# Attention setup in a cross-attention and mixture-of-experts kernel: per-head matrices formed from 64-row operands instead of zero-padded 128-row blocks

## The chip, the cores and the metric

One core of one Trainium2 chip. The metric is the device time of one execution in microseconds. A core has TensorE (PE, matmuls), VectorE (DVE), ScalarE (ACT), GpSimd (POOL) and the DMA queues (SyncE issues most of them). TensorE writes its results to PSUM, eight banks of 128 partitions x 512 fp32; ScalarE and VectorE move them from there to SBUF.

## What is computed

```python
x = x + tanh(g_xattn[0]) * xattn(layernorm(x), ctx, Wq, Wk, Wv, Wo, bo)
x = x + tanh(g_ffn[0]) * ffn(layernorm(x), gate_w, w1, b1, w2, b2)
def xattn(x, context, Wq, Wk, Wv, Wo, bo):     # 16 heads of 64
    q = (x @ Wq); k = (context @ Wk * SCALE); v = (context @ Wv)
    attn = softmax(einsum('bihd,bjhd->bhij', q, k))
    return einsum('bhij,bjhd->bihd', attn, v).reshape(b, n, H * DH) @ Wo + bo
```

x is 2 x 1024 x 256, the context 2 x 64 x 256, everything fp32. The second part is a mixture of eight experts (256 to 1024 to 256, exact gelu), of which each batch element takes two, chosen from the mean of its rows.

## The kernel before

**Setup.** The kernel forms, once, two matrices that fold the projections into the context: A = Wq k^T, per head 256 x 64 for each batch element b, so that the scores are A^T xn; and VW = v Wo, per head 64 x 256 for each b, so that the output is the softmax times VW. The program calls these products *groups*, each of which fills one PSUM bank; `groups` gives their order: `ctxT` (the transposed context), `kT` 0 and 1, `wqT` 0 to 3 (transposes of Wq), `A` 0 to 7, `vT` 0 and 1, `VW` 0 to 7. Everything up to `A` 7 is called early. TensorE, ScalarE and VectorE each walk through this list in the same order (`group` in each engine's block). The early groups use the banks in turn, so that none of the A groups waits for a bank of another A group; the late ones (`vT`, `VW`) use banks 4, 5 and 6 in turn, and a group waits until the bank's previous group has been read (`GRP_BANK`, `GRP_BEFORE`, `wait_group_read`). For `VW` 0 to 7 the previous groups are `A` 7, `vT` 0, `vT` 1, `VW` 0, 1, 2, 3, 4.

**k and v.** A `kT` or `vT` group holds 128 rows (two heads of 64) x 4 head pairs x 2 batch elements x 64 positions. ScalarE evicts the even groups (L426), VectorE the odd ones (L621), each in two pieces of 64 partitions, into `kbd` and `vbd`: blocks of 128x128 of which one diagonal quarter holds head 0 of a pair and the other head 1. The rest is zero; GpSimd writes the zeros at the start (L350, L351), and the evictions wait for that (`zeros_ready`).

**A.** Group i covers half `ct = i // 4` of the 256 rows and two head pairs: two matmuls of a stationary 128x128 piece of `wqT` on a moving 128x256 piece of `kbd` (L936). ScalarE evicts a bank as `a_hi` (L439), rounded to fp32r; VectorE subtracts that from the bank and writes the rest as `a_lo` (L638). Ahead of the eviction of `A` 3 VectorE takes the statistics and the norm of the first half of x (L598 and L575 to L590).

**VW.** Group i covers batch element `b = i // 4` and two head pairs: two matmuls of a stationary 128x128 block of `vbd` on a moving 128x256 piece of `wo_sb` (L944). In the first group of each b a third matmul with one row adds the bias `bo` to head 0: `head0_row` (64 ones and 64 zeros) times `bo_row` (L949). ScalarE evicts the bank scaled by `tg` (L443), VectorE writes the rest (L644). VectorE takes the statistics of the second half of x ahead of `VW` 0.

**Steps.** After the early groups `run_steps` works on 16 tiles of 128 rows of x in a software pipeline: transposes of the normed tile (L1002), scores in three fp32r passes (L902 to L904), maximum (L693), exponentials (L488 and L471), sums (L680), reciprocal (L685), product on GpSimd (L366), transposes (L969), and the product with `vw`. The late groups stand between the steps for s = 0 and s = 1 (`value_groups`). On ScalarE the exponential of tile 0 (L471) comes behind the last `vw` eviction, and on VectorE the sum (L680) behind its own last one. The expert layers follow from 165 us on.

```python
if s == 1:
    value_groups()
...
dve.wait_ge(grp_hi, 8 + i + 1)
```

Of the kernel before, what the change touches and what calls it, by code (L numbers as in the profile page):

```python
# [5 lines left out]
def gated_cross_attention_moe_kernel(nc, x, ctx_tokens, g_xattn, g_ffn, Wq, Wk, Wv, Wo, bo,  # L6
# [5 lines left out]
    ALU = mybir.AluOpType  # L12
    ACT = mybir.ActivationFunctionType
# [3 lines left out]
    P = 128  # L17
    B, S, D = x.shape
    M = ctx_tokens.shape[1]
    HD = Wq.shape[1]  # L20
    DH = 64
# [6 lines left out]
    NP = HD // P  # L28
# [6 lines left out]
    SCALE = DH ** -0.5  # L35
# [46 lines left out]
    ones_row = place("ones_row", [1, P])  # L82
# [2 lines left out]
    b2sel = place("b2sel", [P, B, KD])  # L85
    swt = place("swt", [P, NQ])
    bo_row = place("bo_row", [1, D])
    head0_row = place("head0_row", [1, P])
    warm = place("warm", [1, 2])


# [3 lines left out]
    wv_sb = place("wv_sb", [P, KD, HD], at=first)  # L95
    wo_sb = place("wo_sb", [P, NP, D], at=first)
    wqT = place("wqT", [P, NP, D], at=first)
    kbd = place("kbd", [P, NP, B, P], at=first)
    vbd = place("vbd", [P, NP, B, P], at=first)
    ctx_sb = place("ctx_sb", [P, D], at=first)  # L100
    ctxT = place("ctxT", [P, KD, P], at=first)
    first2 = [cursor[0]]
# [39 lines left out]
    def as_f32(ap):  # L142
        return ap.bitcast(f32)

    stack = ExitStack()
    with stack:
# [99 lines left out]
        for kind, i in groups:  # L246
            who = "act" if kind in ("kT", "wqT", "vT") and i % 2 == 0 else "dve"
            counts[who] += 1
            reader[(kind, i)] = (who, counts[who])

        def wait_group_read(eng, kind, i):

            who, n = reader[(kind, i)]
            eng.wait_ge(grp_act if who == "act" else grp_dve, n)
# [89 lines left out]
        @block.gpsimd  # L344
        def _(pool):
            nc.gpsimd.memset(ident[:, :], 0.0).then_inc(zeros_ready, 1)
            pool.wait_ge(zeros_ready, 1)
            nc.gpsimd.affine_select(out=ident[:, :], in_=ident[:, :], compare_op=ALU.not_equal, fill=1.0,
                                    base=0, pattern=[[-1, P]], channel_multiplier=1).then_inc(ident_ready, 1)
            nc.gpsimd.memset(kbd[:, :, :, :], 0.0).then_inc(zeros_ready, 1)  # L350
            nc.gpsimd.memset(vbd[:, :, :, :], 0.0).then_inc(zeros_ready, 1)  # L351
            nc.gpsimd.memset(ones_row[:, :], 1.0)
            nc.gpsimd.memset(head0_row[:, 0:M], 1.0)
            nc.gpsimd.memset(head0_row[:, M:P], 0.0)
            for e in range(E):
                last = nc.gpsimd.memset(iota_row[:, e:e + 1], float(e))
            last.then_inc(rows_ready, 1)

            def step(s, par):
                t = s - 1  # L360
                if active(t):
                    q = (par - 1) % 2

                    pool.wait_ge(recip_done, t + 1)
                    pr = sx[:, q, :].rearrange("p (h m) -> p h m", m=M)
                    nc.gpsimd.tensor_tensor(pr, pr, rs[:, q, :].unsqueeze(2).broadcast_to([P, H, M]),  # L366
                                            ALU.mult).then_inc(mul_done, 1)
                t = s + LEAD
                if active(t):

                    wait_pos(pool, xT_done, t - 1)
                    tile = xt[:, ds(t, 1), :].rearrange("p o d -> p (o d)")
                    nc.gpsimd.tensor_tensor(xn[:, par, :], tile, mean1[:, ds(t, 1)].broadcast_to([P, D]),
                                            ALU.subtract).then_inc(xc_ready, 1)
                    pool.wait_ge(xc_ready, t + 1)
                    nc.gpsimd.tensor_tensor(xn[:, par, :], xn[:, par, :], rstd1[:, ds(t, 1)].broadcast_to([P, D]),
                                            ALU.mult).then_inc(xn_ready, 1)
            pool.wait_ge(ln_ready, 1)
            run_steps(pool, step)


            pool.wait_ge(ln_ready, 3)
            for t in range(TB, NT):
                pool.wait_ge(yT_done, t - 1)
                nc.gpsimd.tensor_tensor(yb[:, t % 2, :], xt[:, t, :], mean2[:, t:t + 1].broadcast_to([P, D]),
                                        ALU.subtract).then_inc(xc_ready, 1)
                pool.wait_ge(xc_ready, NT + t - TB + 1)
                nc.gpsimd.tensor_tensor(yb[:, t % 2, :], yb[:, t % 2, :], rstd2[:, t:t + 1].broadcast_to([P, D]),
                                        ALU.mult).then_inc(y_ready, 1)

        @block.scalar
        def _(act):
# [24 lines left out]
            def group(kind, i):  # L417
                n = number[(kind, i)]
                bank = ps[:, GRP_BANK[(kind, i)], :]
                if kind in ("kT", "vT") and i % 2 == 0:  # L420
                    act.wait_ge(grp_done, n + 1)
                    act.wait_ge(zeros_ready, 3)
                    dst = kbd if kind == "kT" else vbd
                    for h in range(2):
                        r = slice(h * DH, (h + 1) * DH)
                        last = nc.scalar.activation(  # L426
                            dst[r, 4 * i:4 * i + 4, :, h * M:(h + 1) * M],
                            bank[r, :].rearrange("p (m b j) -> p m b j", m=4, b=B), ACT.Copy,
                            scale=SCALE if kind == "kT" else 1.0)
                    last.then_inc(grp_act, 1)  # L430
                if kind == "wqT" and i % 2 == 0:
                    act.wait_ge(grp_done, n + 1)
                    nc.scalar.activation(wqT[:, 2 * i:2 * i + 2, :],
                                         bank.rearrange("p (m c) -> p m c", m=2), ACT.Copy).then_inc(grp_act, 1)
                if kind == "A":
                    act.wait_ge(grp_done, n + 1)
                    ct, mp = i // 4, i % 4
                    dst = a_hi[:, ct, :].rearrange("p (b m x) -> p m b x", b=B, x=P)[:, 2 * mp:2 * mp + 2, :, :]
                    nc.scalar.activation(dst, bank.rearrange("p (m b x) -> p m b x", m=2, b=B),  # L439
                                         ACT.Copy).then_inc(grp_hi, 1)  # L440
                if kind == "VW":
                    act.wait_ge(grp_done, n + 1)
# [115 lines left out]
        def _(dve):  # L558
# [50 lines left out]
            def group(kind, i):  # L609
# [4 lines left out]
                    nc.vector.tensor_copy(ctxT[:, :, :], bank[:, 0:D].rearrange("p (k i) -> p k i", k=KD)).then_inc(grp_dve, 1)  # L614
                if kind in ("kT", "vT") and i % 2 == 1:
                    dve.wait_ge(grp_done, n + 1)
                    dve.wait_ge(zeros_ready, 3)
                    dst = kbd if kind == "kT" else vbd
                    for h in range(2):
                        r = slice(h * DH, (h + 1) * DH)  # L620
                        last = nc.vector.tensor_scalar(  # L621
                            dst[r, 4 * i:4 * i + 4, :, h * M:(h + 1) * M],
                            bank[r, :].rearrange("p (m b j) -> p m b j", m=4, b=B),
                            SCALE if kind == "kT" else 1.0, None, ALU.mult)
                    last.then_inc(grp_dve, 1)
                if kind == "wqT" and i % 2 == 1:
                    dve.wait_ge(grp_done, n + 1)
                    nc.vector.tensor_copy(wqT[:, 2 * i:2 * i + 2, :],
# [2 lines left out]
                    x_stats(0)  # L631
                    x_norm(0)
                if kind == "A":
                    ct, mp = i // 4, i % 4
                    view = [w[:, ct, :].rearrange("p (b m x) -> p m b x", b=B, x=P)[:, 2 * mp:2 * mp + 2, :, :]
                            for w in (a_hi, a_lo)]
                    dve.wait_ge(grp_hi, i + 1)
                    nc.vector.tensor_tensor(view[1], bank.rearrange("p (m b x) -> p m b x", m=2, b=B),  # L638
                                            as_f32(view[0]), ALU.subtract).then_inc(grp_dve, 1)
                if kind == "VW" and i == 0:  # L640
                    x_stats(1)
                if kind == "VW":
# [253 lines left out]
        def _(pe):  # L896
# [9 lines left out]
            def group(kind, i):  # L906
# [17 lines left out]
                if kind == "wqT":  # L924
                    pe.wait_ge(ld_wq, 16)
                    for m in range(2):
                        for k in range(KD):
                            c0 = (2 * i + m) * P
                            last = nc.tensor.transpose(bank[:, (m * KD + k) * P:(m * KD + k + 1) * P],
                                                       wq_sb[:, k, c0:c0 + P], ident[:, :])  # L930
                if kind == "A":
                    ct, mp = i // 4, i % 4
                    wait_group_read(pe, "kT", mp // 2)
                    wait_group_read(pe, "wqT", mp)
                    for m in range(2):
                        last = mm(bank[:, m * B * P:(m + 1) * B * P], wqT[:, 2 * mp + m, ct * P:(ct + 1) * P],  # L936
                                  kbd[:, 2 * mp + m, :, :].rearrange("p b x -> p (b x)"), start=True, stop=True)
                if kind == "VW":
                    b, mp = i // 4, i % 4
                    pe.wait_ge(ld_wo, 16)  # L940
                    wait_group_read(pe, "vT", mp // 2)
                    for m in range(2):
                        biased = mp == 0 and m == 0
                        last = mm(bank[:, m * D:(m + 1) * D], vbd[:, 2 * mp + m, b, :], wo_sb[:, 2 * mp + m, :],  # L944
                                  start=True, stop=not biased)
                        if biased:
                            pe.wait_ge(rows_ready, 1)
                            pe.wait_ge(ld_small, 64)
                            last = mm(bank[:, 0:D], head0_row[:, :], bo_row[:, :], start=False, stop=True)  # L949
                last.then_inc(grp_done, 1)  # L950
            for g in groups[:EARLY]:
                group(*g)

            wait_group_read(pe, "A", 0)

            def value_groups():
                for g in groups[EARLY:]:
                    group(*g)

            def step(s, par):  # L960
                t = s - 2
# [215 lines left out]
```

## Time and profile before

| | us |
|---|---|
| three runs | 369.66, 371.54, 371.82 |
| median | 371.54 |
| the profiled execution | 371.07 |
| its span | 369.2 |
| setup up to TensorE's last A matmul | 22.5 |
| VW stage on TensorE | 38.4 to 47.4 |

The span runs from the first instruction to the last of the profiled execution. In the rows, `x16` is the count of merged instructions, the first number the start in us, the second the time they cover together. An fp32 matmul is two records. Names such as `a_hi` have their buffer number left out, and in `ps<-kbd,wqT 128*128 128x256` the first pair of numbers is the stationary operand, the second the moving one. The granted clock is a share of 2.4 GHz.

### The profile page before, as it was taken

Reading aid. Unit: us, or ns where it says so; the run is one execution under the profiler, and the core shown is the slowest. Engines: PE = TensorE matmul, PEld = TensorE weight load, DVE = VectorE, ACT = ScalarE, POOL = GpSimd, SP = SyncE. Lnnn points to the kernel's source line nnn. Section 1 sums busy time; section 2 is a strip of 40 time slices with the busy share of each in tenths; the row PEclk is TensorE's granted clock in tenths of the full one; section 3 lists DMA queues with packets and bytes.
Section 4 is the critical chain, followed back from the end, with each engine's and each line's share of the span. In section 5 each row is a group of like instructions: output and inputs, shape, how many; then the busy total and the mean of one; then the engine's idle time right before and its main releaser. Section 6 shows DMA issues by size and latency. Waiting matters only on the chain.

```text
span 369.2 us, 6051 instructions
## 1 busy us (share of the span) xinstructions
PE 339.2 (92%) x1782; PEld 285.5 (77%) x1782; DVE 240.6 (65%) x565; ACT 172.0 (47%) x583; POOL 65.5 (18%) x83
## 2 busy tenths in 40 slices
PE   1958889999999799879979999999999999999994
PEld 1937569989989599769858778888888888888883
DVE  0493789887688798865996882656566366552643
ACT  1433565766756477724355832435463264221420
POOL 5021034535445332210173000000000000000000
PEclk9987999999999899976999998999999999999998
DMA  6930000000000000052500076000000000020011
GB/s 209 369 119 2 1 7 0 2 0 0 0 0 0 1 3 0 2 176 73 210 0 0 2 235 221 2 0 0 0 0 2 1 0 0 17 99 0 1 58 57
DMA packets 12119, 17.22 MB, mean 47 GB/s; under 512 B 945, under 2 KB 10298, under 8 KB 12098
## 3 DMA queue, kind: packets, MB, share of 16 engines
q1 hardware_dynamic: 11536, 16.95, 13.8%
q8 instruction: 11, 0.18, 0.2%
q10 hardware_dynamic: 562, 0.01, 0.1%
q14 instruction: 10, 0.08, 0.1%
HBM read 14.86 MB, written 2.10 MB: 46 GB/s over the span
## 4 chain that ended last, share of the span: by engine, by line
PE 77%; DVE 13%; issue 3%; ACT 2%; DMA 2%; DVEq 1%; POOL 1%; SPq 0%
PE ps L902 22%; PE ps L904 21%; PE ps L903 21%; PE ps L969 4%; PE ps L922 2%; DMA wk_sb<-in_L_xattn_Wk_dram 2%; PE ps L1046 1%; DVE h_lo L866 1%; DVE h_hi L864 1%; PE ps L944 1%; DVE w_lo L877 1%; PE ps L1019 1%; PE ps L1106 1%; PE ps L1002 1%; DVE w_lo L872 1%
## 5 line engine op out<-in xcount | busy, mean ns | idle before, releaser
L532 ACT ACTIVATE gel<-ps,b1sel 128x512 f32<-128x512 f32 x64 | 44.0, 688 | 110.6 <-PE ps L904 110.5
L864 DVE CAST h_hi<-gel 128x512 fp32r<-128x512 f32 x64 | 28.0, 438 | 64.9 <-ACT gel L532 64.5
L902 PE MATMUL ps<-yT_hi,w_hi 128*128 128x512 f32 (+1 forms) x128 | 51.6, 403 | 0.0
L903 PE MATMUL ps<-yT_lo,w_hi 128*128 128x512 f32 (+1 forms) x128 | 51.3, 401 | 0.0
L904 PE MATMUL ps<-yT_hi,w_lo 128*128 128x512 f32 (+1 forms) x128 | 51.2, 400 | 0.0
L902 PE MATMUL ps<-h_hi,w_hi 128*128 128x512 f32 x128 | 50.9, 398 | 0.0
L904 PE MATMUL ps<-h_hi,w_lo 128*128 128x512 f32 x128 | 50.3, 393 | 0.0
L903 PE MATMUL ps<-h_lo,w_hi 128*128 128x512 f32 x128 | 50.3, 393 | 0.0
L866 DVE TENSOR_TENSOR h_lo<-gel,h_hi 128x512 fp32r<-128x512 f32 x64 | 45.5, 711 | 2.2
L366 POOL TENSOR_TENSOR sx<-sx,rs 128x1024 f32<-128x1024 f32 x16 | 30.5, 1904 | 81.7 <-DVE rs L685 81.7
L488 ACT ACTIVATE sx<-ps,mx 128x64 f32<-128x64 f32 x128 | 38.1, 323 | 13.9 <-DVE mx L693 13.9
L902 PE MATMUL ps<-vw,pT_hi 128*128 128x256 f32 (+1 forms) x128 | 38.5, 301 | 1.1 <-DVE pT_lo L671 1.1
L903 PE MATMUL ps<-vw,pT_hi 128*128 128x256 f32 (+1 forms) x128 | 37.1, 290 | 0.0
L904 PE MATMUL ps<-vw,pT_lo 128*128 128x256 f32 (+1 forms) x128 | 37.1, 290 | 0.0
L902 PE MATMUL ps<-a_hi,xT_hi 128*128 128x512 f32 (+1 forms) x64 | 28.0, 438 | 1.5 <-DVE xT_lo L699 1.5
L904 PEld LDWEIGHTS ps<-yT_hi,w_lo 128*128 128x128 f32 x128 | 24.5, 191 | 6.0
L903 PEld LDWEIGHTS ps<-yT_lo,w_hi 128*128 128x128 f32 x128 | 24.5, 191 | 5.5
L902 PEld LDWEIGHTS ps<-yT_hi,w_hi 128*128 128x128 f32 x128 | 24.3, 190 | 5.5
L903 PEld LDWEIGHTS ps<-h_lo,w_hi 128*128 128x128 f32 x128 | 24.1, 188 | 5.3
L902 PEld LDWEIGHTS ps<-h_hi,w_hi 128*128 128x128 f32 x128 | 24.1, 188 | 5.3
L904 PEld LDWEIGHTS ps<-h_hi,w_lo 128*128 128x128 f32 x128 | 24.0, 188 | 5.3
L488 ACT ACTIVATION_READ_ACCUMULATOR sx<-ps,mx 128x1 f32 x128 | 27.6, 215 | 0.0
(136 smaller groups left out, 627.6 us busy)
## 6 DMA issues: line engine op xcount, KB each, us to landing
stage_w<-in_L_ffn_w_dram SPq DMA_DIRECT2D x8, 1024.0 KB, 6.3
xt<-in_x_dram SPq DMA_DIRECT2D x2, 1024.0 KB, 13.0
out_dram<-xt SPq DMA_DIRECT2D x8, 256.0 KB, 2.1
wk_sb<-in_L_xattn_Wk_dram SPq DMA_DIRECT2D x1, 1024.0 KB, 7.2
wq_sb<-in_L_xattn_Wq_dram SPq DMA_DIRECT2D x1, 1024.0 KB, 9.5
wv_sb<-in_L_xattn_Wv_dram SPq DMA_DIRECT2D x1, 1024.0 KB, 14.0
wo_sb<-in_L_xattn_Wo_dram SPq DMA_DIRECT2D x1, 1024.0 KB, 12.1
ctx_sb<-in_ctx_dram SPq DMA_DIRECT2D x1, 128.0 KB, 3.2
```

What stands on the lines that cost most here:

```text
L366: nc.gpsimd.tensor_tensor(pr, pr, rs[:, q, :].unsqueeze(2).broadcast_to([P, H, M]), ALU.mult).then_inc(mul_done, 1)
L488: last = nc.scalar.activation(sx[:, par, c0:c0 + M], ps[:, 2 * par + 1, c0 - BANK:c0 - BANK + M], ACT.Exp, bias=mx[:, par, h:h + 1], accum ...
L532: nc.scalar.activation(gel[:, f % 2, :], ps[:, 4 + f % 2, :], ACT.Gelu, bias=b1sel[:, b, f, slot:slot + 1]).then_inc(gelu_done, 1)
L864: nc.vector.tensor_copy(h_hi[:, f % 4, :], gel[:, f % 2, :]).then_inc(hhi_ready, 1)
L866: nc.vector.tensor_tensor(h_lo[:, f % 4, :], gel[:, f % 2, :], as_f32(h_hi[:, f % 4, :]), ALU.subtract).then_inc(hlo_ready, 1)
L872: nc.vector.tensor_tensor(w1_lo[nxt][:, ds(pc, 1), pf * P:(pf + 1) * P], stage_w1[nxt][:, ds(pc, 1), pf * P:(pf + 1) * P], as_f32(w1_hi[nx ...
L877: nc.vector.scalar_tensor_tensor(w2_lo[nxt][:, pf, ds(pc * P, P)], stage_w2[nxt][:, pf, ds(pc * P, P)], swt[:, q + 1:q + 2], as_f32(w2_hi[ ...
L902: mm(acc, hi_w, hi_x, start=start, stop=False)
L903: mm(acc, hi_w, lo_x, start=False, stop=False)
L904: return mm(acc, lo_w, hi_x, start=False, stop=stop)
L922: last = mm(bank[:, m * P:(m + 1) * P], w_sb[:, k, c0:c0 + P], ctxT[:, k, :], start=(k == 0), stop=(k == KD - 1))
L969: last = nc.tensor.transpose(ps[:, 4 + half, m * P:(m + 1) * P], sx[:, par, c0:c0 + P], ident[:, :])
```

## The change

`kbd` and `vbd`, their zeros, the wait for these and `head0_row` are gone. k and v are evicted in one piece per bank into `kT_sb` and `vT_sb` (partitions 0 to 63 head 0 of each pair, 64 to 127 head 1). A and VW are formed per head: each matmul takes 64 rows, either 0 to 63 or 64 to 127. TensorE works on two groups at a time (`score_pair`, `value_pair`), of which the even one collects heads 0 of the pairs and the odd one heads 1, each in a bank of its own; in VW the two positions within a bank go to output partitions 0 to 63 and 64 to 127. A pair of groups waits for both of its banks first, and signals at its last matmul into either. The order of the heads within a batch element changes with it (`a_part`), the same way in A and VW. The groups, their banks and what each waits for are as before.

```diff
-    kbd = place("kbd", [P, NP, B, P], at=first)
-    vbd = place("vbd", [P, NP, B, P], at=first)
+    kT_sb = place("kT_sb", [P, NP, B, M], at=first)
+    vT_sb = place("vT_sb", [P, NP, B, M], at=first)
...
+        def a_part(w, i):
+
+            ct, half, odd = i // 4, i // 2 % 2, i % 2
+            return w[:, ct, :].rearrange("p (b u m x) -> p u m b x", b=B, u=4, x=M)[:, 2 * half + odd, :, :, :]
...
-            nc.gpsimd.memset(kbd[:, :, :, :], 0.0).then_inc(zeros_ready, 1)
-            nc.gpsimd.memset(vbd[:, :, :, :], 0.0).then_inc(zeros_ready, 1)
             nc.gpsimd.memset(ones_row[:, :], 1.0)
-            nc.gpsimd.memset(head0_row[:, 0:M], 1.0)
-            nc.gpsimd.memset(head0_row[:, M:P], 0.0)
...
                     act.wait_ge(grp_done, n + 1)
-                    act.wait_ge(zeros_ready, 3)
-                    dst = kbd if kind == "kT" else vbd
-                    for h in range(2):
-                        r = slice(h * DH, (h + 1) * DH)
-                        last = nc.scalar.activation(
-                            dst[r, 4 * i:4 * i + 4, :, h * M:(h + 1) * M],
-                            bank[r, :].rearrange("p (m b j) -> p m b j", m=4, b=B), ACT.Copy,
-                            scale=SCALE if kind == "kT" else 1.0)
-                    last.then_inc(grp_act, 1)
+                    dst = kT_sb if kind == "kT" else vT_sb
+                    nc.scalar.activation(dst[:, 4 * i:4 * i + 4, :, :].rearrange("p m b j -> p (m b j)"), bank, ACT.Copy,
+                                         scale=SCALE if kind == "kT" else 1.0).then_inc(grp_act, 1)
...
-                                            as_f32(view[0]), ALU.subtract).then_inc(grp_dve, 1)
+                    nc.vector.tensor_tensor(a_part(a_lo, i), bank.rearrange("p (m b x) -> p m b x", m=4, b=B),
+                                            as_f32(a_part(a_hi, i)), ALU.subtract).then_inc(grp_dve, 1)
...
-                if kind == "A":
-                    ct, mp = i // 4, i % 4
-                    wait_group_read(pe, "kT", mp // 2)
-                    wait_group_read(pe, "wqT", mp)
-                    for m in range(2):
-                        last = mm(bank[:, m * B * P:(m + 1) * B * P], wqT[:, 2 * mp + m, ct * P:(ct + 1) * P],
-                                  kbd[:, 2 * mp + m, :, :].rearrange("p b x -> p (b x)"), start=True, stop=True)
...
+            def two_banks(kind, i):
+
+                banks = []
+                for odd in range(2):
+                    banks.append(ps[:, GRP_BANK[(kind, i + odd)], :])
+                    if GRP_BEFORE[(kind, i + odd)]:
+                        wait_group_read(pe, *GRP_BEFORE[(kind, i + odd)])
+                return banks
+
+            def score_pair(i):
+
+                ct, half = i // 4, i // 2 % 2
+                banks = two_banks("A", i)
+                wait_group_read(pe, "kT", half)
+                wait_group_read(pe, "wqT", 2 * half)
+                wait_group_read(pe, "wqT", 2 * half + 1)
+                for m in range(4):
+                    for odd in range(2):
+                        r = slice(odd * DH, (odd + 1) * DH)
+                        last = mm(banks[odd][:, m * P:(m + 1) * P], wqT[r, 4 * half + m, ct * P:(ct + 1) * P],
+                                  kT_sb[r, 4 * half + m, :, :].rearrange("p b j -> p (b j)"), start=True, stop=True)
+                        if m == 3:
+                            last.then_inc(grp_done, 1)
+
+            def value_pair(i):
+
+                b, half = i // 4, i // 2 % 2
+                banks = two_banks("VW", i)
+                pe.wait_ge(ld_wo, 16)
+                wait_group_read(pe, "vT", half)
+                for c in range(2):
+                    for pos in range(2):
+                        m = 4 * half + 2 * c + pos
+                        for odd in range(2):
+                            r = slice(odd * DH, (odd + 1) * DH)
+                            biased = m == 0 and odd == 0
+                            last = mm(banks[odd][pos * M:(pos + 1) * M, c * D:(c + 1) * D], vT_sb[r, m, b, :],
+                                      wo_sb[r, m, :], start=True, stop=not biased)
+                            if c == 1 and pos == 1:
+                                last.then_inc(grp_done, 1)
+                    if half == 0 and c == 0:
+
+                        pe.wait_ge(rows_ready, 1)
+                        pe.wait_ge(ld_small, 64)
+                        mm(banks[0][0:M, 0:D], ones_row[:, 0:M], bo_row[:, :], start=False, stop=True)
```

VectorE's evictions of the odd `kT` and `vT` groups and ScalarE's of `a_hi` change in the same way.

## Rows read from the trace of the kernel before

**Rows 1.** The page, busy time by engine: us, share of the span, instructions.
```profile
PE 339.2 (92%) x1782; PEld 285.5 (77%) x1782; DVE 240.6 (65%) x565; ACT 172.0 (47%) x583; POOL 65.5 (18%) x83
```

**Rows 2.** Table by stretch: us, busy us (instructions) by engine, granted clock, DMA share, GB/s.
```profile
15.50:22.50 7.00, 6.99 (x33) 5.80 (x31) 6.09 (x16) 4.45 (x8) 0.00 (x0) 1.00 0.95 305
22.50:26.80 4.30, 0.00 (x0) 0.00 (x0) 3.71 (x19) 0.69 (x2) 1.29 (x3) 0.83 0.00 0
...
29.00:31.70 2.70, 2.70 (x7) 2.13 (x8) 0.00 (x0) 0.00 (x0) 0.26 (x1) 0.50 0.02 6
38.40:47.40 9.00, 8.73 (x35) 6.22 (x36) 7.27 (x15) 4.63 (x7) 0.00 (x0) 1.00 0.00 1
52.20:59.10 6.90, 6.85 (x46) 6.19 (x46) 6.08 (x18) 4.90 (x26) 3.13 (x4) 1.00 0.01 2
```

**Rows 3.** Chain that ended last, 8 to 53 us: start, us, what.
```profile
15.58 2.60 PE ps L936 x12
...
25.43 3.08 DVE a_lo L638 x5
...
44.50 3.34 PE ps L944 x14
...
49.25 0.69 DVE sm L680
...
50.29 1.91 POOL sx L366
52.25 0.76 PE ps L969 x5
```

**Rows 4.** Timeline, 0 to 20 us: start, us, engine, line, operation, count, [idle before].
```profile
1.43 1.80 POOL L350 MEMSET kbd<- 128x2048 f32 x1
...
12.08 1.19 ACT L426 ACTIVATE kbd<-ps 64x512 f32<-64x512 f32 x2 [6.28 <-PE ps L922]
...
13.67 1.91 PE L929 MATMUL ps<-ident,wq_sb 128*128 128x128 f32 x16
13.87 1.39 DVE L621 TENSOR_SCALAR kbd<-ps 64x512 f32<-64x512 f32 x2 [8.63 <-PE ps L922]
...
15.29 1.29 DVE L628 COPY wqT<-ps 128x512 f32<-128x512 f32 x2
...
15.41 7.07 PE L936 MATMUL ps<-kbd,wqT 128*128 128x256 f32 x32
...
18.20 0.60 ACT L439 ACTIVATE a_hi<-ps 128x512 fp32r<-128x512 f32 x1 [0.27 <-PE ps L936]
18.83 0.69 DVE L638 TENSOR_TENSOR a_lo<-ps,a_hi 128x512 fp32r<-128x512 f32 x1 [0.17 <-ACT a_hi L439]
...
19.44 2.70 DVE L598 BATCH_NORM_STATS2 stats<-xt  x8
```

**Rows 5.** Timeline, 37 to 49 us.
```profile
37.07 1.21 ACT L426 ACTIVATE vbd<-ps 64x512 f32<-64x512 f32 x2
...
38.42 0.67 PE L944 MATMUL ps<-wo_sb,vbd 128*128 128x256 f32 x2 [1.18 <-ACT vbd L426]
38.77 2.71 DVE L598 BATCH_NORM_STATS2 stats<-xt  x8
...
39.02 0.69 PE L949 MATMUL ps<-bo_row,head_row 1*128 1x256 f32 x2
...
39.65 2.43 PE L944 MATMUL ps<-wo_sb,vbd 128*128 128x256 f32 x10
...
42.32 1.56 PE L944 MATMUL ps<-wo_sb,vbd 128*128 128x256 f32 x6 [0.24 <-DVE vw L644]
43.48 0.69 ACT L443 ACTIVATE vw<-ps,tg 128x512 fp32r<-128x512 f32 x1 [0.69 <-PE ps L944]
...
48.58 0.75 DVE L644 SCALAR_TENSOR_TENSOR vw<-ps,tg,vw 128x512 fp32r<-128x512 f32 x1 [0.22 <-ACT vw L443]
```

**Rows 6.** Timeline of TensorE, 222 to 225 us: narrow moving operands.
```profile
222.69 1.94 PE L1046 MATMUL ps<-hotT,b_sb 8*128 8x2 f32 x16
```

More of the change, by code:

```diff
@@ L87, in gated_cross_attention_moe_kernel @@
     bo_row = place("bo_row", [1, D])
-    head0_row = place("head0_row", [1, P])
     warm = place("warm", [1, 2])
@@ L436, in group @@
                     act.wait_ge(grp_done, n + 1)
-                    ct, mp = i // 4, i % 4
-                    dst = a_hi[:, ct, :].rearrange("p (b m x) -> p m b x", b=B, x=P)[:, 2 * mp:2 * mp + 2, :, :]
-                    nc.scalar.activation(dst, bank.rearrange("p (m b x) -> p m b x", m=2, b=B),
+                    nc.scalar.activation(a_part(a_hi, i), bank.rearrange("p (m b x) -> p m b x", m=4, b=B),
                                          ACT.Copy).then_inc(grp_hi, 1)
@@ L616, in group @@
                     dve.wait_ge(grp_done, n + 1)
[L617 to L625, printed above, removed]
+                    dst = kT_sb if kind == "kT" else vT_sb
+                    nc.vector.tensor_scalar(dst[:, 4 * i:4 * i + 4, :, :].rearrange("p m b j -> p (m b j)"), bank,
+                                            SCALE if kind == "kT" else 1.0, None, ALU.mult).then_inc(grp_dve, 1)
                 if kind == "wqT" and i % 2 == 1:
@@ L633, in group @@
                 if kind == "A":
-                    ct, mp = i // 4, i % 4
-                    view = [w[:, ct, :].rearrange("p (b m x) -> p m b x", b=B, x=P)[:, 2 * mp:2 * mp + 2, :, :]
-                            for w in (a_hi, a_lo)]
                     dve.wait_ge(grp_hi, i + 1)
-                    nc.vector.tensor_tensor(view[1], bank.rearrange("p (m b x) -> p m b x", m=2, b=B),
-                                            as_f32(view[0]), ALU.subtract).then_inc(grp_dve, 1)
+                    nc.vector.tensor_tensor(a_part(a_lo, i), bank.rearrange("p (m b x) -> p m b x", m=4, b=B),
+                                            as_f32(a_part(a_hi, i)), ALU.subtract).then_inc(grp_dve, 1)
                 if kind == "VW" and i == 0:
@@ L930, in group @@
                                                        wq_sb[:, k, c0:c0 + P], ident[:, :])
-                if kind == "A":
-                    ct, mp = i // 4, i % 4
-                    wait_group_read(pe, "kT", mp // 2)
-                    wait_group_read(pe, "wqT", mp)
-                    for m in range(2):
-                        last = mm(bank[:, m * B * P:(m + 1) * B * P], wqT[:, 2 * mp + m, ct * P:(ct + 1) * P],
-                                  kbd[:, 2 * mp + m, :, :].rearrange("p b x -> p (b x)"), start=True, stop=True)
@@ L938, in group @@
[L938 to L949, printed above, removed]
@@ L951, in _ @@
             for g in groups[:EARLY]:
-                group(*g)
+                if g[0] != "A":
+                    group(*g)
+                elif g[1] % 2 == 0:
+                    score_pair(g[1])
             wait_group_read(pe, "A", 0)
@@ L957, in value_groups @@
                 for g in groups[EARLY:]:
-                    group(*g)
+                    if g[0] != "VW":
+                        group(*g)
+                    elif g[1] % 2 == 0:
+                        value_pair(g[1])
             def step(s, par):
```

## The prediction

> **What bounds the kernel now.** I read the page's engine shares first: TensorE is busy for 92% of the span [rows 1]. That is an average, and the change touches only the first 50 us, so the second view was the table by stage [rows 2]. There TensorE is full while A is formed (7.0 us of 7.0, 15.5 to 22.5 us), has no work at all for 4.3 us behind it, and is nearly full in the VW stage (8.7 of 9.0 us) and in the steady steps (6.85 of 6.9). Only the chain of waits says which of these stretches set the end [rows 3]. In the A stage the chain follows TensorE only through the first twelve records (each fp32 matmul is two records), then passes to VectorE: its third `a_lo`, the statistics and norm of the first half of x, and its five remaining `a_lo`, ending at 28.5 us. So the second half of the A matmuls lies beside VectorE's statistics and is on no path. In the VW stage the chain is TensorE's, and it leaves by the last `vw` eviction, VectorE's sum `sm`, GpSimd's product `sx`, and the transposes at 52.25 us. From there TensorE is full [rows 2], and a delay at that point is carried to the end one for one: TensorE, ScalarE and VectorE all take their work in order and have nothing else that they could draw forward.
>
> **Memsets.** Two of 1.80 us on GpSimd, over by 5 us, go [rows 4]. The first eviction that needed the zeros starts at 12.08 us [rows 4]. Worth 0.
>
> **k and v evictions.** Two pieces of 64x512 per bank become one of 128x512. A 64-partition piece takes ScalarE 1.19 / 2 = 0.60 us and VectorE 1.39 / 2 = 0.69 us; the 128-partition evictions of `a_hi` and `wqT` take the same 0.60 and 1.29 / 2 = 0.65 us [rows 4]. So partitions cost nothing, and a bank's eviction halves. For k this is off the path: the chain there is TensorE, from the k matmuls through the transposes [rows 4]. It lets VectorE take its `wqT` at 14.75 instead of 15.29 us, which the change needs, since the first pair of A groups waits for `wqT` 0 and 1. For v it is on the path: TensorE's first VW matmul waits for ScalarE's eviction, 37.07 to 38.28 us, and starts at 38.42 [rows 5]. After: 37.67, and 37.81 us. Gain 0.6 us there, and VectorE's statistics of the second half of x (2.71 us) move from 38.77 to 38.07 and end at 40.8. The long strides of the new `a_hi`/`a_lo` views cost nothing: the k eviction already writes runs of 64 elements at the full rate.
>
> **A.** Sixteen fp32 matmuls of 256 columns become 32 of 64 rows and 128 columns. Now: 7.07 / 32 = 0.22 us a record [rows 4]; a record of 128 columns costs half, 0.11. Two records of one matmul use the same rows of the array and must follow each other; but the second of one can run beside the first of the next, which uses the other rows. Then a matmul costs one record time, a pair of groups 8 x 0.11 = 0.9 us. What matters is when VectorE can begin its third `a_lo` (18.83 us now [rows 4]), since from there to its fourth at 25.43 it works without a gap. TensorE starts at 15.6 (15.41 and one change of the array's shape, 0.19, worked out below); the first pair's first bank is ready at 15.6 + 7 x 0.11 + 0.39 = 16.8 (0.39 from the start of its last record to ScalarE, which is the 0.49 found below for a record of 256 columns, less 0.1 for the shorter one); ScalarE then evicts three banks, 16.8, 17.4, 18.0, ending at 18.6. The second pair, held for `wqT` 3 until 16.3, is done by 17.7, in time. Third `a_lo` at 18.6: 0.2 us earlier. Below it is bounded by ScalarE, so no more than 0.2 can be won however fast TensorE is. Above: the trace has sixteen records that move only two columns and so show the pace of weight loads of 128 columns, 1.94 / 16 = 0.12 us [rows 6]. If two loads can't go at once, 64 loads are 7.7 us, the second pair starts at 17.5, its first bank is ready at 17.5 + 13 x 0.12 + 0.39 = 19.5, and the third `a_lo` starts at 20.1: 1.3 us later. I take -0.2, because the loads go into separate rows as the matmuls do, and keep +1.3 for the range.
> The Trainium skill, page "TensorEngine Tiling (Array Packing)", section "Key Properties", says that different tiles can load weights and multiply in parallel; by it the A term is the -0.2. No row here shows two tiles at work.
>
> **VW.** Sixteen matmuls of 256 columns (and two of the bias) become 32, on 64 rows and 64 columns each, in four quadrants. One record of 256 columns is 0.222 us, as in A. The four of group 3 start from 42.32, and ScalarE's eviction follows at 43.48 [rows 5]: 3 x 0.222, and 0.49 from the last record's start. Alone, one after another, the new 64 records are 14.2 us; all four quadrants at once 3.6 us. I take 7.1: quadrants are issued in program order, two records each, so that one matmul's second record overlaps the next one's first and no more. TensorE's sum is thus unchanged, and what decides is the order. The bias keeps its price, 2 x 0.213 and a pause on either side: from the first matmul's two records at 38.42 to the bias at 39.02 are 0.60 us, to the next at 39.65 another 0.63; two records fill 0.43 of each, and some 0.19 are left over each time [rows 5]. In all 0.81 us, at the first and third pair.
> A pair now fills two banks and both are finished only at its end, out of three banks. The pair (2,3) needs the bank of group 0, so it waits for VectorE's read of it; (4,5) for the read of 2; (6,7) for the read of 4. Before, group 3 waited for 0, 4 for 1 and so on, with the group between at work: TensorE waited 0.2 us there. Now nothing runs beside an eviction. From a pair's start: first bank ready for ScalarE after 7 x 0.222 + 0.49 = 2.05 (2.86 with bias); ScalarE 0.69 us, VectorE starts 0.03 behind it, 0.75 us, TensorE 0.06 later [rows 5].
> Pair 0: TensorE 37.81, ScalarE 40.7 and 41.4, VectorE 41.4 to 42.2. Pair 1: TensorE 42.2, ScalarE 44.3, VectorE 45.0 to 45.8. Pair 2: TensorE 45.8, ScalarE 48.7, VectorE 49.4 to 50.2. Pair 3: TensorE 50.2, ScalarE 52.3 and 53.0, the last `vw` on VectorE 53.7. It is at 48.58 now [rows 5]: +5.1 us. Pauses of TensorE of about 1.7 us stand between pairs.
> The Trainium skill, page "TensorE: Matmul & The Clock Gate", section "The mechanism" of Part 3, says that matmuls start and end in program order, without reordering; by it the VW sum stays 7.1, not 3.6. The page "TensorEngine Tiling (Array Packing)", "Key Properties", says that a change of tiling mode drains the engine; the trace agrees at the bias, 0.19 us each way.
>
> **Sum.** The profiled execution: 371.07 us, span 369.2. 371.07 - 0.2 + 5.1 = 376.0 us. The median of the runs, 371.54, lies 0.47 above it; on that scale 376.4. What measurement can tell from no change is about 1%, 3.7 us.
>
> **Rivals.**
> (a) Weight loads of two row groups don't overlap: A +1.3 instead of -0.2, 371.5 + 5.1 + 1.3 = 377.9 us. For it: the load pace of 0.12, the same for 8 rows as it would be for 64. Against: that pace is of loads into the same rows, where the second has to wait anyway.
> (b) Not slower: all four quadrants of VW work together. A pair's first bank is then ready after 0.67 + 0.49 = 1.16 us (1.97 with bias). VectorE reads group 0 at 40.8 (its statistics), the pairs start at 37.8, 41.6, 44.3 and 47.8, the last `vw` at 50.4, +1.8; with A -0.2, 373.1 us, inside 1%. It decides from the point where a pair takes TensorE under 1.2 us instead of 1.8. For it: each quadrant has cells and an output range of its own. Against: two records per matmul on the same quadrant, in order. To be level, a pair would have to cost almost nothing.
> (c) The change doesn't do what it says: narrow matmuls run one by one. VW 14.2 us: a pair's first bank after 13 x 0.222 + 0.49 = 3.4 us; the last `vw` at 59.0, +10.4; A +1.3: 383.2 us. For it: the trace shows no two matmuls at once.
> (d) The granted clock falls in the pauses of VW. It was 1.00 until TensorE had been idle for some 2.8 us, then 0.50 (a mean of 0.83 over 22.5 to 26.8 [rows 2]). The new pauses are 1.7 us. If it falls, three pairs take 7 x 0.21 = 1.5 us more each: 381 us.
> The first scores ran at 0.50 [rows 2] behind the idle time of the A stage; TensorE is idle there after the change as well, for longer, so I count 0, give or take 1 us for when the clock comes back.
>
> **How the numbers follow.** Forecast 42%, (a) 18%, (b) 20%, (c) 9%, (d) 4%, and 7% for a gain from something not seen here. The range 372.6 to 380.0 holds the forecast, (a) and (b). (c), (d) and the gain, 20%, are outside. The forecast's own range is 375.2 to 377.6. Slower by over 1% (above 375.3): the forecast less a small part, (a), (c), (d), 69%. Within 1%: (b) and that part, 24%. Faster: 7%.
>
> **What the profile would show.** Right: A's 64 records in about 4 us, with VectorE's third `a_lo` near 18.6; v evicted in 0.60 us; VW's first record near 37.8, TensorE waiting for VectorE's `vw` three times, 1.7 us each, and the last `vw` near 53.7; the steps behind it as long as now. Wrong: A over 7 us (a); 16 records of a VW pair within 1 us (b) or 3.5 us (c); a granted clock under 1.00 in VW (d). If TensorE doesn't wait for `vw` between the pairs, or the step behind VW absorbs the delay, the main term is wrong.

## The result and the profile after

376.72 us in the median of four runs, beside 371.3 for the kernel before on the same chip: ratio 1.0143, 95% interval 1.0098 to 1.0189. A second measurement, told below, gave 1.0126. The profiled execution took 377.56 us, the slowest of the four (the fastest took 376.0), its span 375.4. The forecast was 376.4, slower. The ratios leave out runs more than 1.5% above the fastest of the same kernel: that takes out five of the twelve runs of the group-by-group kernel below, which lie at 374.3 to 375.2 us, but not the similar ones of the kernel before, at about 374 (four of the 35 beside the first experiments, eight of the 23 beside the later ones), and no trace of such a run was kept.

The table by stretch of the kernel after (us, busy us and instructions of TensorE, its weight loads, VectorE, ScalarE, GpSimd, then granted clock, DMA share, GB/s):

```profile
44.00:46.00 2.00, 0.39 (x8) 0.22 (x8) 1.04 (x2) 1.26 (x2) 0.00 (x0) 0.65 0.00 0
46.00:50.00 4.00, 3.04 (x18) 0.69 (x15) 0.56 (x2) 0.91 (x2) 0.00 (x0) 0.50 0.01 4
50.00:54.00 4.00, 3.34 (x19) 2.04 (x20) 1.81 (x3) 1.67 (x4) 0.00 (x0) 0.50 0.02 8
```

Beside [rows 2]: TensorE is busy for 0.4 of 2 us and then for some 3 of 4 where it was nearly full, and the granted clock falls within the VW stage, from 1.00 to 0.50 (0.65 is the mean of the stretch in which it fell). It was 1.00 throughout that stage before.

The timeline of the kernel after, 12 to 56 us, all engines:

```profile
12.30 0.60 ACT L423 ACTIVATE kT_sb<-ps 128x512 f32<-128x512 f32 x1 [8.06 <-PE ps L905]
...
14.92 0.69 DVE L610 TENSOR_SCALAR kT_sb<-ps 128x512 f32<-128x512 f32 x1 [9.66 <-PE ps L905]
...
16.60 3.68 PEld L935 LDWEIGHTS ps<-kT_sb,wqT 64*128 64x128 f32 x64 [0.21 <-DVE wqT L614]
16.63 3.84 PE L935 MATMUL ps<-kT_sb,wqT 64*128 64x128 f32 x64
...
18.42 1.89 DVE L621 TENSOR_TENSOR a_lo<-ps,a_hi 128x512 fp32r<-128x512 f32 x3 [1.06 <-ACT a_hi L431]
20.23 2.70 DVE L590 BATCH_NORM_STATS2 stats<-xt  x8
...
38.53 0.64 ACT L423 ACTIVATE vT_sb<-ps 128x512 f32<-128x512 f32 x1
...
39.30 0.66 PE L952 MATMUL ps<-wo_sb,vT_sb 64*64 64x256 f32 x8 [0.62 <-ACT vT_sb L423]
...
39.90 0.64 PE L960 MATMUL ps<-bo_row,ones_row 1*64 1x256 f32 x2
...
41.18 1.27 ACT L435 ACTIVATE vw<-ps,tg 128x512 fp32r<-128x512 f32 x2 [2.02 <-PE ps L952]
...
43.10 1.09 PE L952 MATMUL ps<-wo_sb,vT_sb 64*64 64x256 f32 x16 [1.97 <-DVE vw L627]
44.24 1.26 ACT L435 ACTIVATE vw<-ps,tg 128x512 fp32r<-128x512 f32 x2 [1.79 <-PE ps L952]
44.96 1.41 DVE L627 SCALAR_TENSOR_TENSOR vw<-ps,tg,vw 128x512 fp32r<-128x512 f32 x2 [1.30 <-ACT vw L435]
...
45.81 1.13 PE L952 MATMUL ps<-wo_sb,vT_sb 64*64 64x256 f32 x8 [1.61 <-DVE vw L627]
...
49.09 1.27 ACT L435 ACTIVATE vw<-ps,tg 128x512 fp32r<-128x512 f32 x2 [3.59 <-PE ps L952]
...
50.66 1.98 PE L952 MATMUL ps<-wo_sb,vT_sb 64*64 64x256 f32 x16 [1.62 <-DVE vw L627]
...
53.41 1.41 DVE L627 SCALAR_TENSOR_TENSOR vw<-ps,tg,vw 128x512 fp32r<-128x512 f32 x2 [2.19 <-ACT vw L435]
```

k is evicted in 0.60 and 0.69 us instead of 1.19 and 1.39 [rows 4], v by ScalarE in 0.64 instead of 1.21 [rows 5]. A's 64 records take 3.84 us; its 32 of twice the columns took 7.07. The VW stage reads as a ladder: a pair on TensorE (43.10), two evictions by ScalarE (44.24), VectorE's two behind them (44.96), and, once the first of VectorE's two has read its bank, the next pair (45.81). From the first VW record to the last `vw` eviction it was 10.2 us (38.42 to 48.58 [rows 5]); now it is 14.8 (39.30 to 54.1, the second of the two that begin at 53.41).

The chain that ended last, of the kernel after, 8 to 60 us:

```profile
8.48 6.40 PE ps L905 x32
...
43.10 1.15 PE ps L952 x16
44.26 0.68 ACT vw L435
44.96 0.76 DVE vw L627
45.81 1.13 PE ps L952 x8
46.94 1.04 PE ps L960 x2
```

Between pairs it runs over ScalarE and VectorE, as forecast. Its first line is the k matmuls, 6.40 us. In the chain of the kernel before they took 5.33:

```profile
8.50 5.33 PE ps L922 x32
```

In both kernels TensorE's first records take twice the time of the later ones. Before, 14 of them stand in the 3.10 us from 8.50 on and 21 in the 2.10 us from 11.70 on; in this execution the slow ones reach to 13.80 (25 records in 5.30 us), and the k matmuls end 1.05 us later. That is no effect of the change (the second measurement's profiled execution has VectorE's k eviction at 14.05, 0.87 us earlier than this one), but it has to be taken off every time read here against before. A further 0.65 us stands in the first scores, which run at a granted clock of 0.50 at first in both kernels: from the first of them to the v matmuls it was 4.52 us (28.99 to 33.51), now it is 5.17 (29.78 to 34.95), and 4.73 in the second measurement's execution. The forecast counted 0 for it, give or take 1 us; whether the change has a part in it isn't shown.

Behind the last pair the chain doesn't leave as forecast, by the last `vw`. The second tile's scores stand behind that pair on TensorE, and the chain goes through them (at half clock at first) to VectorE's maximum of that tile. Its line in the chain of the kernel after, and the same maximum in the timeline of the kernel before:

```profile
56.67 1.24 DVE mx L676
```

```profile
50.63 1.23 DVE L693 TENSOR_REDUCE mx<-ps 128x16 f32<-128x1024 f32 x1 [0.42 <-PE ps L904]
```

This maximum is 6.04 us later than before. GpSimd's product of the first tile, which hangs on the last `vw`, is 5.48 later (55.77 against 50.29 [rows 3]). The maxima of the later tiles are 6.0 to 6.1 us late (the twelfth at 122.97 against 116.92), so what is carried to the end is the delay of the scores.

### The profile page after: what moved, and what is told of

It reads as the page before. It is cut to its first block, busy times and chain, and to the rows that moved or that the text cites. A ratio compares the mean times of both kernels' runs of the same rounds, so it can differ in the third digit from the quotient of the medians.

```text
span 375.4 us, 6169 instructions
## 1 busy us (share of the span) xinstructions
PE 338.4 (90%) x1846; PEld 282.4 (75%) x1846; DVE 238.7 (64%) x563; ACT 169.8 (45%) x581; POOL 61.8 (16%) x79
## 4 chain that ended last, share of the span: by engine, by line
PE 76%; DVE 14%; ACT 3%; issue 3%; DMA 2%; DVEq 1%; POOL 1%; SPq 0%
PE ps L885 21%; PE ps L886 21%; PE ps L887 21%; PE ps L985 3%; PE ps L905 3%; DMA wk_sb<-in_L_xattn_Wk_dram 2%; PE ps L952 1%; PE ps L1062 1%; DVE h_lo L849 1%; DVE h_hi L847 1%; ACT sx L480 1%; DVE a_lo L621 1%; DVE w_lo L860 1%; PE ps L1035 1%; DVE stats L590 1%
```

## The experiments

**A alone.** VW, v and its zeros stay as before; A is written in the old order of heads.

```diff
-            for g in groups[:EARLY]:
-                group(*g)
+            for g in groups[:EARLY]:
+                if g[0] != "A":
+                    group(*g)
+                elif g[1] % 2 == 0:
+                    score_pair(g[1])
```

> A formed as in the change (k evicted whole, no zero blocks for k, 64-row pairs), VW and v as before. Theory P (the whole loss is in the VW stage: pairs held back by three banks, and the clock that falls in their pauses): the third a_lo comes 0.2 to 0.3 us earlier relative to the k eviction, VW stage as before, so about 371.1 us, ratio 0.999. Rival R (the A part costs as well, because TensorE is idle for longer behind it and its clock comes back later in the first scores, 4.6 us instead of 2.9): 0.5 to 1.5 us slower than before, about 372.3 us, ratio 1.003.

Measured: 369.93 us beside 370.54, ratio 0.9991 (0.9954 to 1.0028). The timeline of this kernel, first VW matmul and last `vw`:

```profile
38.31 0.67 PE L944 MATMUL ps<-wo_sb,vbd 128*128 128x256 f32 x2 [1.19 <-ACT vbd L434]
...
48.47 0.75 DVE L651 SCALAR_TENSOR_TENSOR vw<-ps,tg,vw 128x512 fp32r<-128x512 f32 x1 [0.22 <-ACT vw L449]
```

Both 0.11 us earlier than in [rows 5]. The A part costs nothing in the trace and gives about what was forecast there; the interval doesn't exclude a gain or a loss of 1 us, but the loss of 5 us is elsewhere.

**VW group by group.** Everything of the change is kept, but the pair is split into its two groups, on the same three banks.

```diff
+            def value_one(i):
+                b, half, odd = i // 4, i // 2 % 2, i % 2
+                bank = ps[:, GRP_BANK[("VW", i)], :]
+                wait_group_read(pe, *GRP_BEFORE[("VW", i)])
...
-                    elif g[1] % 2 == 0:
-                        value_pair(g[1])
+                    else:
+                        value_one(g[1])
```

> The changed kernel, but VW formed group by group as before: the four matmuls of the even group, then those of the odd one, each signalled and waited for alone, on the same three banks and quadrants. Theory P: TensorE and the evictions overlap again; a group's four matmuls use two column halves of the same rows and take 0.9 us or less, so the stage is at least as fast as before, the v eviction saves 0.6 us: 370.3 us, ratio 0.998; granted clock 1.00 in the stage. Rival Q (64-row, 64-column fp32 matmuls and their changes of the array's shape are what costs): stays near 376 us.

Measured: 369.84 us beside 370.54, ratio 0.9956 (0.9929 to 0.9983), so the loss is gone. The profiled execution took 369.73 us, against 371.07 before. Its timeline:

```profile
38.32 0.65 PE L951 MATMUL ps<-wo_sb,vT_sb 64*64 64x256 f32 x4 [0.62 <-ACT vT_sb L423]
...
39.47 1.51 PE L951 MATMUL ps<-wo_sb,vT_sb 64*64 64x256 f32 x20
...
42.07 1.31 PE L951 MATMUL ps<-wo_sb,vT_sb 64*64 64x256 f32 x12 [1.09 <-DVE vw L627]
...
47.96 0.75 DVE L627 SCALAR_TENSOR_TENSOR vw<-ps,tg,vw 128x512 fp32r<-128x512 f32 x1 [0.59 <-ACT vw L435]
```

Twenty records follow each other from 39.47, through three groups, while ScalarE evicts; the stage is 9.6 us long (38.32 to 47.96) instead of 14.8, its granted clock 1.00. The 64-row matmuls and the quadrants are the same as in the changed kernel. So neither is what cost the time. It was the unit in which they were waited for, together with the clock that fell in the waits (Filler, below).

**Five banks.** The changed kernel, pairs and all, with two more banks for VW.

```diff
-        GRP_BANK = {g: n % 8 if n < EARLY else 4 + (n - EARLY) % 3 for n, g in enumerate(groups)}
+        LATE_BANKS = [4, 5] + [2, 3, 6, 4, 5, 2, 6, 4]
+        GRP_BANK = {g: n % 8 if n < EARLY else LATE_BANKS[n - EARLY] for n, g in enumerate(groups)}
...
+                if isinstance(s, int) and s == 1:
+                    wait_group_read(pe, "VW", 5)
```

> The changed kernel with VW's groups in five banks instead of three (2 to 6; the second tile's scores then wait for the read of group 5). Theory P: TensorE no longer waits for a pair's evictions, ScalarE's eight evictions of 0.64 to 0.69 us follow each other without a gap from 1.9 us after the stage's start and the last vw comes some 3 us earlier than in the kernel before: 368 us, ratio 0.991. Rival Q: 374 to 376 us.

Measured: 370.19 us beside 370.54, ratio 0.9982 (0.9957 to 1.0008). The loss is gone here too, by the other way of taking the wait out; a gain isn't shown. Its timeline:

```profile
37.69 0.66 PE L953 MATMUL ps<-wo_sb,vT_sb 64*64 64x256 f32 x8 [0.62 <-ACT vT_sb L424]
...
41.49 0.66 PE L953 MATMUL ps<-wo_sb,vT_sb 64*64 64x256 f32 x8 [1.11 <-DVE vw L628]
...
44.09 2.73 DVE L628 SCALAR_TENSOR_TENSOR vw<-ps,tg,vw 128x512 fp32r<-128x512 f32 x4 [0.72 <-ACT vw L436]
```

The last `vw` begins at 46.1 (the fourth of those from 44.09), 2.5 us earlier than before; I had expected some 3. The third pair still waits for the read of group 0, which comes behind VectorE's statistics. The profiled execution is faster by 2.1 us (368.99 beside 371.07), and the second tile's maximum is 2.0 earlier (48.61), but the median of twelve runs, from 368.13 to 371.58, is lower by only 0.35. What the other runs lost is open: only one of them has a trace.

**Filler.** The changed kernel with matmuls in the pauses, whose results nobody reads.

```diff
                         value_pair(g[1])
+                        if g[1] < 6:
+                            for _ in range(FILL):
+                                mm(ps[:, 3, :], xT_hi[:, 0, 0, :], a_hi[:, 0, 0:BANK], start=True, stop=True)
```

> The changed kernel with six more matmuls of 128x512 behind each of the first three VW pairs, into a bank that the next scores overwrite; they lie in TensorE's pauses of 2 us. Theory P with the clock: the granted clock stays 1.00 through the stage, pairs 2 and 3 and the second tile's scores run at full rate, 2 to 3 us less than the changed kernel: 374.2 us. Rival (the clock is beside the chain): no less than the changed kernel, 376.7 us, or more by the changes of shape.

Measured: 373.54 us beside 370.54, ratio 1.0065 (1.0034 to 1.0095). More work made the kernel faster, by about 2.5 us against the changed one (1.0143 and 1.0126 against 1.0065). Its timeline, and its table by stretch:

```profile
41.38 1.09 PE L953 MATMUL ps<-wo_sb,vT_sb 64*64 64x256 f32 x16 [0.39 <-DVE vw L628]
...
42.40 1.66 PE L978 MATMUL ps<-a_hi,xT_hi 128*128 128x512 f32 x6
...
47.54 1.09 PE L953 MATMUL ps<-wo_sb,vT_sb 64*64 64x256 f32 x16
...
49.40 1.41 DVE L628 SCALAR_TENSOR_TENSOR vw<-ps,tg,vw 128x512 fp32r<-128x512 f32 x2 [1.30 <-ACT vw L436]
```

```profile
38.00:46.00 8.00, 7.58 (x64) 3.88 (x58) 5.21 (x12) 2.56 (x5) 0.00 (x0) 1.00 0.00 1
46.00:52.00 6.00, 5.76 (x36) 3.94 (x36) 3.98 (x7) 3.18 (x6) 0.23 (x1) 1.00 0.04 11
```

The filler (1.66 us) ends before the next pair may start, so it changes no wait; pairs take 1.09 us, the last one too (1.98 in the changed kernel), and the clock is granted at 1.00 throughout. What is left, 2.4 us over the kernel before (1.3 to 3.5 by the interval), is the ladder at full clock. The profiled execution, the fastest of the twelve, has less of it: the last `vw` is at 50.1 us, 1.5 behind [rows 5], and the second tile's maximum at 51.63, 1.0 behind.

**Quadrant by quadrant.** The changed kernel with the loops inside a pair turned; the bias stands directly behind the matmul that it is added to.

```diff
-                for m in range(4):
-                    for odd in range(2):
+                for odd in range(2):
+                    for m in range(4):
...
-                for c in range(2):
-                    for pos in range(2):
-                        for odd in range(2):
+                for odd in range(2):
+                    for pos in range(2):
+                        for c in range(2):
```

> The changed kernel with the order inside a pair turned: in A all four matmuls on rows 0 to 63 first, then those on rows 64 to 127; in VW both matmuls of a quadrant behind each other, quadrant after quadrant. It is for the pace of TensorE's records. Theory N (narrow operands work at once only with other tiles): on one row half A's records fall from 0.06 to 0.11 us each, and VW's four records of one quadrant to 0.11 us each or more, from 0.055. Rival M (a narrow record is itself shorter and no two tiles are needed): the same 0.06 and 0.055 us in any order.

One execution, 377.88 us. Its timeline, all A records, the second VW pair and ScalarE's eviction behind it:

```profile
16.62 5.01 PE L935 MATMUL ps<-kT_sb,wqT 64*128 64x128 f32 x64
...
43.09 1.12 PE L952 MATMUL ps<-wo_sb,vT_sb 64*64 64x256 f32 x16 [1.58 <-DVE vw L627]
44.21 1.26 ACT L435 ACTIVATE vw<-ps,tg 128x512 fp32r<-128x512 f32 x2 [1.43 <-PE ps L952]
```

Then TensorE alone, within three short windows: 16.60 to 17.14 us, 39.20 to 39.70, and 43.05 to 43.14.

```profile
16.62 0.68 PE L935 MATMUL ps<-kT_sb,wqT 64*128 64x128 f32 x4
```

```profile
39.28 0.61 PE L952 MATMUL ps<-wo_sb,vT_sb 64*64 64x256 f32 x2 [0.61 <-ACT vT_sb L423]
```

```profile
43.09 0.47 PE L952 MATMUL ps<-wo_sb,vT_sb 64*64 64x256 f32 x4 [1.58 <-DVE vw L627]
```

A fell from 0.06 to 0.08 us a record, not to 0.11, and VW stayed: 16 records in 1.12 us instead of 1.09. Neither theory as written. But in VW four records start within 0.05 us (third window), although the first four of the program belong to one quadrant. And the pair's first bank, whose matmuls are the first half of the program's, is ready for ScalarE only at 44.21, when all 16 records are through. In the group-by-group kernel, where at the end only two quadrants have work left, the last records start two at a time; in this line of its timeline the two stand alone, after 40.78 us:

```profile
40.60 0.38 PE L951 MATMUL ps<-wo_sb,vT_sb 64*64 64x256 f32 x2
```

One quadrant alone is seen too: ahead of the bias of the first pair only one matmul stands, and its two records start 0.24 us apart (second window: 0.61 us for two, where the two side by side took 0.38). A's first records are those of one row half alone: four start by 17.14 us, where the changed kernel, with both halves at work from 16.63, has started eight by then. So a record of 256 columns takes its 0.22 us in its quadrant (0.11 us of 128 columns in its row half), only one at a time there, and TensorE takes work for an idle quadrant from further down its queue than program order. The trace doesn't name a record's quadrant; this is the reading that fits all three orders.

**The changed kernel again.**

> The changed kernel once more, beside the others on the same chip: 376.7 us by the first measurement, ratio 1.014.

Measured: 376.4 us beside 371.25, ratio 1.0126 (1.0069 to 1.0182). The granted clock fell in the VW stage in this execution as well: 1.00 over 38 to 42 us, 0.50 over 42.8 to 50.

**No bias.** The changed kernel without the two bias products (the output lacks `bo`).

```diff
-                            biased = m == 0 and odd == 0
+                            biased = False
...
-                        mm(banks[0][0:M, 0:D], ones_row[:, 0:M], bo_row[:, :], start=False, stop=True)
```

> The changed kernel without the product of ones and bo (the output lacks the bias of the attention). Both bias products lie on the chain of their pair; two pauses and two records each, 0.7 us at full clock, 1.5 to 2 us in all, and if TensorE's clock falls as in the changed kernel, no more than that: 375.0 us, ratio 1.010. Rival: the bias lies beside the statistics of x at the first pair and is worth 0.7 us at most.

Measured: 375.34 us beside 371.25, ratio 1.0095 (1.0056 to 1.0133): 1.1 us less than the changed kernel beside it, though the two intervals overlap. Its timeline:

```profile
39.84 1.09 PE L952 MATMUL ps<-wo_sb,vT_sb 64*64 64x256 f32 x16 [0.62 <-ACT vT_sb L423]
39.95 2.94 DVE L590 BATCH_NORM_STATS2 stats<-xt  x8
40.97 1.26 ACT L435 ACTIVATE vw<-ps,tg 128x512 fp32r<-128x512 f32 x2 [1.28 <-PE ps L952]
42.80 1.39 DVE L627 SCALAR_TENSOR_TENSOR vw<-ps,tg,vw 128x512 fp32r<-128x512 f32 x2
...
46.34 1.99 PE L952 MATMUL ps<-wo_sb,vT_sb 64*64 64x256 f32 x16 [1.62 <-DVE vw L627]
48.37 1.27 ACT L435 ACTIVATE vw<-ps,tg 128x512 fp32r<-128x512 f32 x2 [2.34 <-PE ps L952]
```

The first pair is ready 0.75 us earlier (1.13 us from its start to ScalarE's eviction, 1.88 with bias), but VectorE is with the statistics until 42.8 and takes `vw` no sooner: worth nothing, as the rival has it. The second bias lies in the stretch at half clock and is worth 1.25 us (45.81 to 49.09 is 3.28, here 46.34 to 48.37 is 2.03), more than the rival's 0.7 in all. So the total was about right with the wrong split.

**Group by group and five banks.** Both edits above together.

> Both repairs together: VW group by group, and in five banks. Theory P: the stage is then bound by the evictions, eight of 0.64 us on ScalarE and 0.66 us on VectorE; TensorE's wait of 1 us in the middle of the stage with five banks goes: 0.5 to 1 us less than five banks alone, 369.5 us, ratio 0.996. Rival: the bound is elsewhere and it is level with five banks alone.

Measured: 369.55 us beside 371.25, ratio 0.9936 (0.9902 to 0.997). That is the lowest ratio here and clear of 1, but its interval overlaps those of the two repairs alone, so by the times it isn't shown to be faster than either. Its timeline:

```profile
41.40 3.73 ACT L436 ACTIVATE vw<-ps,tg 128x512 fp32r<-128x512 f32 x6 [1.99 <-PE ps L952]
42.53 5.36 DVE L628 SCALAR_TENSOR_TENSOR vw<-ps,tg,vw 128x512 fp32r<-128x512 f32 x8
```

All eight of VectorE's `vw` evictions follow each other from the end of the statistics (42.53, 5.36 us for eight), and the statistics follow VectorE's own v eviction at 39.07. The stage's path lies on VectorE; TensorE no longer sets its pace. From ScalarE's v eviction to the second tile's maximum it is 10.9 us (38.78 to 49.67), 11.7 with five banks alone (36.91 to 48.61), 12.7 group by group (37.54 to 50.19) and 13.6 in the kernel before (37.07 to 50.63).

## Why the prediction was right, and where not

- **Time and side**: 376.4 forecast, 376.7 measured. The place was right: the VW stage, its pairs, its three banks. The two kernels that take out the wait, group by group and with five banks, show it.
- **k, v, memsets**: right. v's eviction is 0.64 instead of 0.60 us, and from its start to the first VW record it is 0.77 us (38.53 to 39.30) instead of 1.35 (37.07 to 38.42), 0.58 gained.
- **A**: -0.2 forecast. From the end of the k matmuls to the start of the statistics of x it is 5.35 us (14.88 to 20.23) against 5.61 (13.83 to 19.44): -0.26. The weight loads of two row halves do go at once, 64 of them in 3.68 us where one at a time takes 0.12 [rows 6], and rival (a) falls. The Trainium skill says ("TensorEngine Tiling (Array Packing)", "Key Properties") that different tiles load and multiply in parallel. The trace agrees: 64 loads and 64 matmuls of 128 columns in 3.84 us.
- **VW, the step that failed**: "quadrants are issued in program order, two records each, so that one matmul's second record overlaps the next one's first and no more", 7.1 us of records. TensorE did all four quadrants at once, 16 records in four rounds of 0.22 us, 0.9 us instead of 1.8 (1.09 with the tail of the last), and a pair's first bank was ready after 1.14 us. That is rival (b), and its price was about right: +1.8 forecast for the last `vw`, +1.5 in the filler kernel, which has full clock. The rule of the Trainium skill that the forecast cited ("TensorE: Matmul & The Clock Gate", Part 3, "The mechanism"), that matmuls start strictly in program order, doesn't hold here: four records start within 0.05 us when the program's first four are in one quadrant.
- **The clock, the second miss**: rival (d) was given 4%, because the pauses (1.7 us) were shorter than the 2.8 us after which the clock had fallen before. It fell at about 44.6 us (0.65 over 44 to 46), 0.4 us behind the end of the second pair. The pauses in front of it were 2.0 and 1.6 us, and the pair between them kept TensorE busy for 1.1 us instead of the forecast's 1.8 and more; that this made the fall likelier is argued, not shown. Half rate then cost the third and fourth pair and the second tile's scores some 2.5 us, as the filler shows.
- **The way out of the stage, a third miss**: the last `vw`, `sm`, `sx` and the transposes were to carry the delay to the end one for one. The transposes came 5.48 us late, the second tile's maximum 6.04, and the steps behind follow the maximum.
- **Sum by the runs**: A -0.3 (0.9991), the ladder at full clock +2.7 (1.0065 less that), the clock +2.6 (1.0134, the mean of the two measurements, less 1.0065): +5.0 us. The traces split it otherwise. From ScalarE's v eviction to the second tile's maximum it is 13.56 us before (37.07 to 50.63), 14.83 in the filler kernel (36.80 to 51.63), and 17.92 and 18.14 in the two executions of the changed kernel (37.21 to 55.13, 38.53 to 56.67): the ladder +1.3, the clock +3.1 to +3.3. The intervals are too wide to choose between the two.
- **Luck**: the forecast had -0.2 and +5.1 in one term. The total was right because two misses cancelled, a ladder 2.4 us too long (3.8 by the traces) and 2.6 us of clock (3.1 to 3.3) that was counted at nothing. Had the clock stayed up, the result would have been 373.7, inside the range and within 1%.
- **The bias**: forecast 0.81 us at a pair. It is 0.75 (1.88 less 1.13) at full clock and 1.25 at half; at the first pair it hides behind the statistics.

## What to carry to other kernels

When a step is made faster by working on two buffers as a unit, count the buffers: a unit of two out of three leaves no room to overlap with the evictions, and the engine that was sped up stops instead. Keep the signal and the wait at the smallest unit whatever the order of the work, and give a faster producer more buffers. An engine whose work is halved but whose partners are not will pause, and on TensorE a pause can cost twice, as it did here: once as such and once by the clock that falls in it. And look at what stands behind the stage on the engine that was held up: here the second tile's scores, not the last result of the stage, handed the delay on.

## What was not expected of the hardware

- Narrow matmuls ran in four quadrants at once in both orders in which a pair was tried: 16 records of 64 rows, 64 columns of weights and 256 moving columns in 0.9 us, and in 1.09 to 1.12 with the tail. The two row halves of A slow down only from 0.06 to 0.08 us a record when the program has eight records of one half first.
- The granted clock fell to 0.50 with no idle time of TensorE longer than 2 us in the stage in front of it, and was still 0.50 over 50 to 54 us, though TensorE was busy for 3.34 of these 4. It fell in all four traces of kernels with pairs, three banks and no filler (the changed one's two, quadrant by quadrant, no bias), and in no other VW stage.
- The pause at a change from 64-row quadrants to a one-row matmul is some 0.15 us: 39.30 to 39.90 us less eight records, of which four run at once, is 0.16; from the full array it was 0.17 and 0.20.
